# One layer norm's residual factor, made by GpSimd in a later step

## The chip, the cores and the metric

The kernel runs on one core of a Trainium2 chip. Its engines each have a queue of their own and meet only at semaphores: TensorE (PE; its weight loads are shown apart as PEld), VectorE (DVE), ScalarE (ACT), GpSimd (POOL) and SyncE (SP), which only issues DMAs. The metric is the device time of one execution in microseconds (us), as the median of several runs.

## The reference

The input is 32 sequences of 256 tokens with 128 values each. What is computed, cut to what matters:

```python
x = layernorm(x + attention(x))            # 16 heads of 64, causal softmax, output projection
mu, var = mean(x), var(x)                  # inside the second part, per token
xn = (x - mu) * rsqrt(var + 1e-5) * gamma + beta
probs = softmax(xn @ router_w.T / 1.5)     # 8 experts, the best two are kept
y = sum over the two experts: prob * (silu(xn @ W1[e]) @ W2[e])
out = layernorm(y + x)                     # x is the residual
```

The first layer norm and the one inside the second part are merged in the kernel: what goes to the experts is the doubly normed row z. The residual x is z times a factor for each token, which is worked out from the variance alone. This factor is what the change moves.

## The kernel before, in words

The kernel has three stretches: the attention, sequence by sequence (up to about 980 us), the experts on gathered blocks of 256 rows, and the last layer norm. Each engine's program is written out by hand, in order. In the attention every engine loops over n, the sequence (0 to 31), and q, the step (0 to 3), with d = 4n + q; a step treats two pairs of heads. There is no scheduler: what stands in `step(n, q, d)` of an engine is done in that order, and waits are semaphore counts.

The names that matter:

- PE, in a step: the scores of both pairs (L1292, L1295) into the PSUM banks ps_s, then projections for the next step (L1270), then the transposes of the step before's probabilities (L1313), again into ps_s. A pair's scores wait for two things: for ACT to have evacuated the pair's queries and keys (`qk_done`), and for the transposed probabilities that lie in the same bank to have been copied out (`pt_first_done`, `pt_second_done`).
- DVE: the masked maxima of the scores (L965, L969), the scaling of the probabilities by their reciprocal sums (L981 with 256 and L982 with 128 columns, both from SBUF to SBUF), and copies of transposed probabilities out of PSUM. In the last step of a sequence (q = 3) DVE copies the first pair's (L1149), in the other steps the second pair's (L1082).
- ACT: the exponentials (L691, L694), the evacuation of queries and keys (L680, L681), the copy of the attention outputs `ot` (L724), and in the last step the copy of the second pair's transposed probabilities (L773).
- POOL: in steps 0 and 2 it splits the outputs of two earlier steps into a rounded part (cast, L585, after ACT's copy L724) and a rest (L590). Between the first cast and the first L590 it waits for this step's scores. In step 0 it then works out the tokens' places among the experts (`slots`) and issues two indirect DMAs that send rows z to the experts' queues (L562). In step 1 it adds the bias to the input (L577) and sends the other two. In step 3 it waits for the statistics from DVE (L1049) and norms the rows (`norm`, L505 to L525).

`norm(n)` ends with two big instructions that write z (L517) and release `z_done`, and then four small ones that make the factor: a power (L520), two products (L521, L523) and the product that writes it into the KEEP column of z (L525), with `keep_done`. Each has 128 partitions by 2 elements. `send_tokens` waits for `keep_done`, one sequence behind.

Of the kernel before, what the change touches and what calls it, by code (L numbers as in the profile page):

```python
# [31 lines left out]
def postln_block(nc, x, wq, wk, wv, bq, bk, bv, wo, bo, gamma, beta, router_wt, w1, w2, out):  # L32
    SEQS, S, D = x.shape
# [26 lines left out]
    with ExitStack() as ctx:  # L60
# [6 lines left out]
        def sem(name):  # L67
            return ctx.enter_context(nc.semaphore(name))
# [213 lines left out]
        ln_link = sem("ln_link")  # L282
# [174 lines left out]
        def _(pool):  # L457
# [38 lines left out]

            LINKS = 8

            def norm(n):

                link = lambda k: (n - 1) * LINKS + k
                par = (n - 1) % 2
                mean, var = mv[:, :, 0], mv[:, :, 1]
                pool.wait_ge(mv_done, n)
                pool.tensor_scalar(ln_b[:], var, 1.0 + EPS, EPS * EPS, ALU.mult, ALU.add).then_inc(ln_link, 1)  # L505
                pool.tensor_tensor(ln_negmean[:], mean, neg_one[:, 0:TILES], ALU.mult).then_inc(ln_link, 1)
                pool.tensor_tensor(ln_a[:], var, eps_sb[:, 0:TILES], ALU.add).then_inc(ln_link, 1)
                pool.wait_ge(ln_link, link(3))
                pool.tensor_tensor(ln_r12[:], ln_b[:], neg_half[:, 0:TILES], ALU.pow).then_inc(ln_link, 1)
                if n >= 3:  # L510
                    pool.wait_ge(tokens_sent[par], (n - 1 - par) * (TILES * TOP * 8))
                pool.tensor_tensor(z[:, par, :, TOK], z[:, par, :, TOK], two_seqs[:], ALU.add)
                pool.wait_ge(ln_link, link(4))
                pool.tensor_tensor(ln_shift_z[:], ln_negmean[:], ln_r12[:], ALU.mult).then_inc(ln_link, 1)
                pool.wait_ge(ln_link, link(5))
                for i in range(TILES):
                    ins = pool.tensor_scalar(z[:, par, i, 0:D], res[:, i, :], ln_r12[:, i:i + 1],  # L517
                                             ln_shift_z[:, i:i + 1], ALU.mult, ALU.add)
                ins.then_inc(z_done, 1)
                pool.tensor_tensor(ln_r1[:], ln_a[:], neg_half[:, 0:TILES], ALU.pow).then_inc(ln_link, 1)  # L520
                pool.tensor_tensor(ln_br[:], ln_b[:], ln_r12[:], ALU.mult).then_inc(ln_link, 1)  # L521
                pool.wait_ge(ln_link, link(6))
                pool.tensor_tensor(ln_r1neg[:], ln_r1[:], neg_two[:], ALU.mult).then_inc(ln_link, 1)  # L523
                pool.wait_ge(ln_link, link(8))
                pool.tensor_tensor(z[:, par, :, KEEP], ln_br[:], ln_r1neg[:], ALU.mult).then_inc(keep_done, 1)  # L525

            def slots(n):
                pool.wait_ge(ranks_done, n - 1)
                for i in range(TILES):
                    ins = pool.tensor_tensor(slot_part[:, i], chosen[:, i],  # L530
                                             slot_if[:, i].unsqueeze(1).to_broadcast([P, TOP, E]), ALU.mult)
                ins.then_inc(slot_part_done, 1)
                pool.wait_ge(slot_part_done, n - 1)
                half = slot_part[:].rearrange("p i k (a e) -> p (i k) a e", a=2)
                pool.tensor_tensor(slot_four[:], half[:, :, 0], half[:, :, 1], ALU.add).then_inc(slot_link, 1)
                pool.wait_ge(slot_link, (n - 2) * 2 + 1)
                half = slot_four[:].rearrange("p k (a e) -> p k a e", a=2)
                pool.tensor_tensor(slot_two[:], half[:, :, 0], half[:, :, 1], ALU.add).then_inc(slot_link, 1)
                pool.wait_ge(slot_link, (n - 2) * 2 + 2)
                pool.tensor_tensor(slot_f[:].rearrange("p i k -> p (i k)"), slot_two[:, :, 0], slot_two[:, :, 1], ALU.add  # L540
                                   ).then_inc(slot_f_done, 1)
                pool.wait_ge(slot_f_done, n - 1)
                if n >= 4:
                    pool.wait_ge(tokens_sent[n % 2], (n - 2 - n % 2) * (TILES * TOP * 8))
                pool.tensor_copy(slot_now[:, n % 2, :], slot_f[:].rearrange("p i k -> p (i k)"))
                pool.wait_ge(z_done, n - 1)
                pool.tensor_copy(z[:, n % 2, :, SLOT], slot_f[:, :, 1])
                pool.wait_ge(gates_done, n - 1)
                pool.tensor_copy(z[:, n % 2, :, GATE], gates[:, :, 0])
                pool.tensor_tensor(z[:, n % 2, :, MORE], gates[:, :, 1], gates[:, :, 0], ALU.subtract  # L550
                                   ).then_inc(slots_done, 1)

            def send_tokens(n, i):
                par = n % 2
                if i == 0:
                    pool.wait_ge(slots_done, n - 1)
                    pool.wait_ge(keep_done, n - 1)
                    if n == SEQS - 1:
                        pool.wait_ge(tails_zeroed, 16 * E)
                for k in range(TOP):  # L560
                    col = i * TOP + k
                    pool.indirect_dma_start(  # L562
                        queue, bass.IndirectOffsetOnAxis(ap=slot_now[:, par, col:col + 1], axis=0),
                        z[:, par, i, :], None).then_inc(tokens_sent[par], 16)

            def rest_of_w1(e):
                pool.wait_ge(w1_hi_done, e + 1)
                pool.tensor_tensor(weights[:, W1_LO + e * HID:W1_LO + (e + 1) * HID], w1_raw[:, e], w1_part[:, e % 2],
                                   ALU.subtract).then_inc(w1_lo_done, 1)

            def residual_input(n):
                pool.wait_ge(bo_done, 1)
                if n >= 2:
                    pool.wait_ge(res_done, n - 1)
                pool.wait_ge(x_loaded[(n - 1) % 2], ((n - 1) // 2 + 1) * 16)
                for i in range(TILES):
                    ins = pool.tensor_tensor(xb[:, i, :], x_raw[:, (n - 1) % 2, i, :], bo_sb[:], ALU.add)  # L577
                ins.then_inc(xb_done, 1)

            def round_outputs(s):  # L580
                m, first = s // QUADS, s % QUADS * 2
                pool.wait_ge(ot_done, s + 1)
                if m >= 1:
                    pool.wait_ge(out_half_ready, 2 * m - (1 if first < 4 else 0))
                pool.tensor_copy(ot_hi[:, first:first + 2, :], ot[:, s % 2]).then_inc(ot_hi_done, 1)  # L585

            def rest_of_outputs(s):
                first = s % QUADS * 2
                pool.wait_ge(ot_hi_done, s + 1)
                pool.tensor_tensor(ot_lo[:, first:first + 2, :], ot[:, s % 2], ot_hi[:, first:first + 2, :].bitcast(F32),  # L590
                                   ALU.subtract).then_inc(ot_lo_done, 1)
# [7 lines left out]
            def step(n, q, d):  # L599
                if q in (0, 2) and n in MID:  # L600
                    round_outputs(d - 4)
                    pool.wait_ge(scores_ready, d * 2 + 1)
                    rest_of_outputs(d - 4)
                    round_outputs(d - 3)
                    rest_of_outputs(d - 3)
                if q == 0 and n - 1 in LATE:
                    slots(n - 1)
                    send_tokens(n - 1, 0)
                if q == 1 and n in MID:
                    pool.wait_ge(scores_ready, d * 2 + 1)  # L610
                    residual_input(n)
                if q == 1 and n - 1 in LATE:
                    send_tokens(n - 1, 1)
                if q == 3 and 2 <= n <= E + 1:
                    pool.wait_ge(scores_ready, d * 2 + 1)
                    rest_of_w1(n - 2)
                if q == 3 and n in MID:
                    norm(n)

            pool.wait_ge(small_loaded, 16 * 5)  # L620
            split_projection()
            sequences(step)
            for s in range(LAST - 4, LAST - 2):
                round_outputs(s)
# [5 lines left out]
                rest_of_outputs(s)  # L630
            residual_input(SEQS)
            send_tokens(SEQS - 1, 1)
            norm(SEQS)
            slots(SEQS)
            for i in range(TILES):
                send_tokens(SEQS, i)
# [24 lines left out]
            for f in range(FINS):  # L661
                par = f % 2
# [1009 lines left out]
```

## Time and profile before

| what | value |
|---|---|
| median of 3 runs | 1296.25 us (1296.0 to 1296.68) |
| the profiled execution's own time | 1294.77 us |
| its span in the profile | 1293.0 us |
| PE busy | 1268.1 us, 98% |
| ACT busy | 1136.9 us, 88% |
| DVE busy | 1038.6 us, 80% |
| POOL busy | 750.9 us, 58% |
| chain of work that ended last | PE 93%, ACT 2%, DVE 2%, DMA 2% |

How to read it: the span is what the profile covers, and the execution's own time holds a little around it. Busy shares are means over the three stretches. The chain follows the work back from the last instruction, at each step to what released it. In rows of a timeline the first number is the start in us from the span's beginning, the second the duration; several instructions of one line in a row are merged (x2). What is in brackets is the idle time of the engine before the row, and whose end released it. An instruction may start while the one before it on its engine is still finishing.

### The profile page before, as it was taken

What the parts mean: (1) busy time and instruction counts of PE and PEld (TensorE: products, weight loads), DVE (VectorE), ACT (ScalarE), POOL (GpSimd) and SP (SyncE); (2) the same over time, 40 slices, a digit from 0 to 9 for tenths busy, and PEclk for the clock granted to TensorE, in tenths of its full rate; (3) what the DMA queues carried; (4) which work ended last, traced back from release to release, by engine and by line L of the source; (5) the groups of instructions that cost most, each with busy time, mean ns of one, the idle gap of its engine ahead of it and who ended that gap; (6) DMA issues with size and microseconds to landing.
All of it is one profiled execution on the core that took longest, in us unless ns stands there. A gap on an engine that the chain in (4) does not pass through costs nothing.

```text
span 1293.0 us, 36146 instructions
## 1 busy us (share of the span) xinstructions
PE 1268.1 (98%) x11106; PEld 1125.8 (87%) x11106; DVE 1038.6 (80%) x5179; ACT 1136.9 (88%) x3514; POOL 750.9 (58%) x1333
## 2 busy tenths in 40 slices
PE   7999999999999999999999999999998999999997
PEld 6888888888888888888888888888886999999993
DVE  7888888888888888888888888888897765555537
ACT  7899999998998999889989999989887899999947
POOL 2246666666555565555665665555556676555545
PEclk9999999999999999999999999999999999999999
DMA  5000000000000000000000000000032233222228
GB/s 211 6 14 22 23 22 22 23 23 25 21 16 15 14 14 15 14 14 15 14 14 14 15 15 14 16 17 20 17 145 94 69 86 89 76 81 76 68 82 336
DMA packets 49213, 60.96 MB, mean 47 GB/s; under 512 B 8304, under 2 KB 35059, under 8 KB 48768
## 3 DMA queue, kind: packets, MB, share of 16 engines
q1 hardware_dynamic: 39376, 41.44, 9.9%
q0 software_dynamic: 8640, 17.13, 4.0%
q8 instruction: 93, 1.52, 0.5%
q14 instruction: 96, 0.79, 0.2%
q10 hardware_dynamic: 1008, 0.08, 0.1%
HBM read 30.72 MB, written 28.81 MB: 46 GB/s over the span
## 4 chain that ended last, share of the span: by engine, by line
PE 93%; ACT 2%; DVE 2%; DMA 2%; issue 1%; SPq 0%; POOL 0%; ACTq 0%; POOLq 0%; DVEq 0%
PE ps_a L1270 15%; PE ps_s L1313 13%; PE ps_s L1292 11%; PE ps_s L1270 8%; PE ps_f L1348 7%; PE ps_b L1305 7%; PE ps_f L1305 6%; PE ps_b L1564 5%; PE ps_a L1564 5%; PE ps_s L1295 4%; PE ps_b L1270 4%; PE ps_f L1270 3%; PE ps_s L1629 2%; PE ps_a L1369 1%; PE ps_s L1323 1%
## 5 line engine op out<-in xcount | busy, mean ns | idle before, releaser
L691 ACT ACTIVATE f_y<-f_y,neg_max 128x256 f32<-128x256 f32 x512 | 256.4, 501 | 46.8 <-DVE neg_max L965 46.7
L965 DVE CUSTOM_DVE_ANT_0 f_y<-ps_s,mask 128x256 f32<-128x256 f32 x512 | 214.6, 419 | 60.8 <-PE ps_s L1295 60.5
L1270 PE MATMUL ps_a<-xt_hi,weights 128*128 128x256 f32 x1024 | 240.2, 298 | 0.1
L590 POOL TENSOR_TENSOR ot_lo<-f_y,ot_hi 128x512 fp32r<-128x512 f32 x128 | 165.0, 1289 | 115.2 <-PE ps_s L1295 110.0
L981 DVE TENSOR_SCALAR f_y<-f_y,inv_sums 128x256 f32<-128x256 f32 x512 | 196.5, 384 | 7.0
L694 ACT ACTIVATE f_y<-f_y,neg_max 128x128 f32<-128x128 f32 x512 | 199.8, 390 | 0.0
L1313 PE MATMUL ps_s<-ident,f_y 128*128 128x128 f32 x1536 | 195.2, 273 | 0.0
L656 POOL DMA_INDIRECT y_tok<-f_y,m_dest x142 | 141.7, 998 | 84.8 <-DVE m_dest L1168 56.1
L1270 PEld LDWEIGHTS ps_a<-xt_hi,weights 128*128 128x128 f32 x1024 | 174.5, 188 | 16.0 <-issue 10.9
L1292 PE MATMUL ps_s<-qk 64*128 64x256 f32 x1024 | 176.4, 421 | 5.2 <-ACT qk L681 2.3
L1313 PEld LDWEIGHTS ps_s<-ident,f_y 128*128 128x128 f32 x1536 | 171.4, 141 | 4.9 <-issue 0.3
L982 DVE TENSOR_SCALAR f_y<-f_y,inv_sums 128x128 f32<-128x128 f32 x512 | 158.2, 309 | 0.0
L562 POOL DMA_INDIRECT queue<-z,slot_now x128 | 128.8, 1006 | 35.9 <-issue 26.1
L969 DVE CUSTOM_DVE_ANT_0 f_y<-ps_s,mask 128x128 f32<-128x128 f32 x512 | 146.5, 286 | 0.0
L1270 PE MATMUL ps_a<-xt_lo,weights 128*128 128x256 f32 x512 | 143.1, 279 | 0.0
L680 ACT ACTIVATE qk<-ps_a,bq_sb 128x256 f32<-128x256 f32 x256 | 119.3, 466 | 21.0 <-PE ps_a L1270 21.0
L1270 PE MATMUL ps_s<-m_xhi,weights 128*128 128x256 f32 x568 | 119.8, 293 | 3.1 <-DVE m_xlo L1193 1.8
L681 ACT ACTIVATE qk<-ps_a,bk_sb 128x256 f32<-128x256 f32 x256 | 119.3, 466 | 0.0
L585 POOL CAST ot_hi<-f_y 128x512 fp32r<-128x512 f32 x128 | 78.8, 616 | 62.9 <-ACT f_y L724 62.9
L1292 PEld LDWEIGHTS ps_s<-qk 64*128 64x128 f32 x1024 | 77.6, 185 | 37.9 <-issue 28.7
L1295 PEld LDWEIGHTS ps_s<-qk 64*128 64x128 f32 x1024 | 99.9, 187 | 10.9
L1295 PE MATMUL ps_s<-qk 64*128 64x128 f32 x1024 | 99.9, 271 | 0.0
(230 smaller groups left out, 3365.9 us busy)
## 6 DMA issues: line engine op xcount, KB each, us to landing
m_x<-queue SPq DMA_DIRECT2D x71, 133.0 KB
f_y<-y_tok SPq DMA_DIRECT2D x32, 256.0 KB, 6.8
queue<-empty SPq DMA_DIRECT2D x8, 532.0 KB, 3.8
x_raw<-in_x SPq DMA_DIRECT2D x32, 128.0 KB
out_x<-f_y SPq DMA_DIRECT2D x16, 256.0 KB, 6.3
y_tok<-f_y,m_dest POOLq DMA_INDIRECT x142
f_y<-in_w SPq DMA_DIRECT2D x1, 2048.0 KB, 11.7
m_w<-in_w SPq DMA_DIRECT2D x1, 2048.0 KB, 14.7
```

Source lines behind the costliest of these rows:

```text
L590: pool.tensor_tensor(ot_lo[:, first:first + 2, :], ot[:, s % 2], ot_hi[:, first:first + 2, :].bitcast(F32), ALU.subtract).then_inc(ot_lo_d ...
L691: act.activation(row[:, 0:2 * P], row[:, 0:2 * P], ACT.Exp, scale=-1.0, bias=neg_max[:, pair, h, 0:1], accum_out=sums[:, d % 2, pair, h, 0:1])
L694: act.activation(row[:, 2 * P:3 * P], row[:, 2 * P:3 * P], ACT.Exp, scale=-1.0, bias=neg_max[:, pair, h, 1:2], accum_out=sums[:, d % 2, pa ...
L965: dve.tensor_tensor_reduce(out=row[:, 0:2 * P], in0=ps_s[:, pair, h, 0:2 * P], in1=mask[:].rearrange("p a b -> p (a b)"), scale=-1.0, scal ...
L969: dve.tensor_tensor_reduce(out=row[:, 2 * P:3 * P], in0=ps_s[:, pair, h, 2 * P:3 * P], in1=mask[:, 1, :], scale=-1.0, scalar=-MASKED, op0= ...
L981: dve.tensor_scalar(row[:, 0:2 * P], row[:, 0:2 * P], inv_sums[:, d % 2, pair, h, 0:1], None, ALU.mult)
L982: ins = dve.tensor_scalar(row[:, 2 * P:3 * P], row[:, 2 * P:3 * P], inv_sums[:, d % 2, pair, h, 1:2], None, ALU.mult)
L1270: ins = pe.matmul(dst, lhs, rhs, start=(i == 0), stop=(i == len(terms) - 1))
L1292: pe.matmul(ps_s[:, pair, h, 0:2 * P], qk[r, pair, 0, P:2 * P], qk[r, pair, 1, :], start=True, stop=True)
L1295: ins = pe.matmul(ps_s[:, pair, h, 2 * P:3 * P], qk[r, pair, 0, 0:P], qk[r, pair, 1, 0:P], start=False, stop=True, skip_group_check=True)
L1305: ins = pe.matmul(dst_bank[r, cols], v[:, k, c * P + h * DH:c * P + (h + 1) * DH], pt[:, s % 2, pair, h, src], start=(k == 0), stop=(k == ...
L1313: ins = pe.transpose(ps_s[:, pair, h, dst:dst + P], probs[:, buf, pair, h, src:src + P], ident[:])
```

## The change

The four small instructions that make the factor leave `norm(n)` and become a function `keep_factor(n)`. In the loop POOL calls it for the sequence before in step 1, behind the second pair of DMA issues. After the loop it is called for norm 31 behind `send_tokens(SEQS - 1, 1)`, and for norm 32, the last, directly behind it, as before. The semaphore counts are the same. No other engine's program is changed.

```diff
             def norm(n):
-
-                link = lambda k: (n - 1) * LINKS + k
                 par = (n - 1) % 2
...
                 for i in range(TILES):
                     ins = pool.tensor_scalar(z[:, par, i, 0:D], res[:, i, :], ln_r12[:, i:i + 1],
                                              ln_shift_z[:, i:i + 1], ALU.mult, ALU.add)
                 ins.then_inc(z_done, 1)
+
+            def keep_factor(n):
+                par = (n - 1) % 2
+                pool.wait_ge(ln_link, link(n, 5))
                 pool.tensor_tensor(ln_r1[:], ln_a[:], neg_half[:, 0:TILES], ALU.pow).then_inc(ln_link, 1)
                 pool.tensor_tensor(ln_br[:], ln_b[:], ln_r12[:], ALU.mult).then_inc(ln_link, 1)
-                pool.wait_ge(ln_link, link(6))
+                pool.wait_ge(ln_link, link(n, 6))
                 pool.tensor_tensor(ln_r1neg[:], ln_r1[:], neg_two[:], ALU.mult).then_inc(ln_link, 1)
-                pool.wait_ge(ln_link, link(8))
+                pool.wait_ge(ln_link, link(n, 8))
                 pool.tensor_tensor(z[:, par, :, KEEP], ln_br[:], ln_r1neg[:], ALU.mult).then_inc(keep_done, 1)
...
                 if q == 1 and n - 1 in LATE:
                     send_tokens(n - 1, 1)
+                if q == 1 and n >= 2:
+                    keep_factor(n - 1)
...
             send_tokens(SEQS - 1, 1)
+            keep_factor(SEQS - 1)
             norm(SEQS)
+            keep_factor(SEQS)
             slots(SEQS)
```

The lines of POOL's program below the norm have numbers higher by 6 in the changed kernel up to the loop (the cast is L591 there, the rest L596, the sending DMA L568), and the factor's four are L526 to L531.

In POOL's program at the end of a sequence's last step and the start of the next sequence's first, before:

```order
L514 TENSOR_TENSOR ln_shift_z<-ln_negmean,ln_r12 128x2
L517 TENSOR_SCALAR z<-res,ln_r12,ln_shift_z 128x128 x2
L520 TENSOR_TENSOR ln_r1<-ln_a,neg_half 128x2
L521 TENSOR_TENSOR ln_br<-ln_b,ln_r12 128x2
L523 TENSOR_TENSOR ln_r1neg<-ln_r1,neg_two 128x2
L525 TENSOR_TENSOR z<-ln_br,ln_r1neg 128x2
L585 CAST ot_hi<-f_y 128x512
L590 TENSOR_TENSOR ot_lo<-f_y,ot_hi 128x512
L585 CAST ot_hi<-f_y 128x512
```

And the same place in the changed kernel:

```order
L516 TENSOR_TENSOR ln_shift_z<-ln_negmean,ln_r12 128x2
L519 TENSOR_SCALAR z<-res,ln_r12,ln_shift_z 128x128 x2
L591 CAST ot_hi<-f_y 128x512
L596 TENSOR_TENSOR ot_lo<-f_y,ot_hi 128x512
L591 CAST ot_hi<-f_y 128x512
```

The cast follows directly on the instructions that write z.

In POOL's program in the second step of a sequence, from the DMA issues that send rows to the cast of the third step, before:

```order
L562 DMA queue<-z,slot_now 67840x133 x2
L577 TENSOR_TENSOR xb<-x_raw,bo_sb 128x128 x2
L562 DMA queue<-z,slot_now 67840x133 x2
L585 CAST ot_hi<-f_y 128x512
L590 TENSOR_TENSOR ot_lo<-f_y,ot_hi 128x512
```

And the same place in the changed kernel:

```order
L568 DMA queue<-z,slot_now 67840x133 x2
L583 TENSOR_TENSOR xb<-x_raw,bo_sb 128x128 x2
L568 DMA queue<-z,slot_now 67840x133 x2
L526 TENSOR_TENSOR ln_r1<-ln_a,neg_half 128x2
L527 TENSOR_TENSOR ln_br<-ln_b,ln_r12 128x2
L529 TENSOR_TENSOR ln_r1neg<-ln_r1,neg_two 128x2
L531 TENSOR_TENSOR z<-ln_br,ln_r1neg 128x2
L591 CAST ot_hi<-f_y 128x512
L596 TENSOR_TENSOR ot_lo<-f_y,ot_hi 128x512
```

The four stand between the last DMA issue and the next cast.

## Rows read from the trace of the kernel before

**Rows 1.** Table of stretches: each engine's busy us and its instructions.

```profile
340.00:950.00 610.00, 610.00 (x5494) 532.81 (x5492) 533.94 (x2657) 548.61 (x1875) 354.54 (x697) 1.00 0.05 15
```

**Rows 2.** Waits, 340 to 980 us: us in total, times, longest.

```profile
POOL ot_lo L590 <- PE ps_s L1295: 74.1, 42, 2.2
```

**Rows 3.** Line 1149: duration ns min/median/max, and who waited for it.

```profile
L1149 DVE COPY pt<-ps_s x31: 945/950/954, 37.9 to 953.8; 128x768 f32<-128x768 f32 x31
...
  PE ps_s L1292: 0.8, 2
```

**Rows 4.** Timeline of POOL, 371 to 391 us.

```profile
371.86 0.69 POOL L520 TENSOR_TENSOR ln_r<-ln_a,neg_half 128x2 f32<-128x2 f32 x1
...
373.22 0.61 POOL L585 CAST ot_hi<-f_y 128x512 fp32r<-128x512 f32 x1
375.19 1.28 POOL L590 TENSOR_TENSOR ot_lo<-f_y,ot_hi 128x512 fp32r<-128x512 f32 x1 [1.36 <-PE ps_s L1295]
...
385.33 0.96 POOL L562 DMA_INDIRECT queue<-z,slot_now  x1 [0.30 <-issue]
387.55 0.61 POOL L585 CAST ot_hi<-f_y 128x512 fp32r<-128x512 f32 x1 [1.27 <-ACT f_y L724]
390.38 1.27 POOL L590 TENSOR_TENSOR ot_lo<-f_y,ot_hi 128x512 fp32r<-128x512 f32 x1 [2.22 <-PE ps_s L1295]
```

**Rows 5.** Timeline of ACT, 371 to 375 us.

```profile
371.60 0.57 ACT L724 ACTIVATE f_y<-ps_b 128x512 f32<-128x512 f32 x1
...
374.43 0.47 ACT L681 ACTIVATE qk<-ps_a,bk_sb 128x256 f32<-128x256 f32 x1
```

**Rows 6.** Timeline of DVE, 372 to 389 us.

```profile
372.21 0.28 DVE L982 TENSOR_SCALAR f_y<-f_y,inv_sums 128x128 f32<-128x128 f32 x1
372.41 0.35 DVE L981 TENSOR_SCALAR f_y<-f_y,inv_sums 128x256 f32<-128x256 f32 x1
...
372.87 0.95 DVE L1149 COPY pt<-ps_s 128x768 f32<-128x768 f32 x1
...
387.55 0.70 DVE L982 TENSOR_SCALAR f_y<-f_y,inv_sums 128x128 f32<-128x128 f32 x1
...
388.71 0.94 DVE L1082 COPY pt<-ps_s 128x768 f32<-128x768 f32 x1
```

**Rows 7.** Timeline of PE, 374 to 391 us.

```profile
374.17 0.70 PE L1292 MATMUL ps_s<-qk 64*128 64x256 f32 x4
...
374.95 0.70 PE L1292 MATMUL ps_s<-qk 64*128 64x256 f32 x4
...
375.81 0.73 PE L1270 MATMUL ps_b<-weights,xt_hi 128*128 128x512 f32 x2
...
390.14 0.70 PE L1292 MATMUL ps_s<-qk 64*128 64x256 f32 x4
```

**Rows 8.** Timeline of ACT at the end of sequence 0.

```profile
36.29 0.58 ACT L724 ACTIVATE f_y<-ps_b 128x512 f32<-128x512 f32 x1
```

**Rows 9.** Timeline of POOL, same place.

```profile
36.93 0.72 POOL L585 CAST ot_hi<-f_y 128x512 fp32r<-128x512 f32 x1 [20.89 <-ACT f_y L724]
```

**Rows 10.** Timeline of DVE, same place.

```profile
36.90 0.28 DVE L982 TENSOR_SCALAR f_y<-f_y,inv_sums 128x128 f32<-128x128 f32 x1
37.09 0.70 DVE L981 TENSOR_SCALAR f_y<-f_y,inv_sums 128x256 f32<-128x256 f32 x1
...
37.91 0.95 DVE L1149 COPY pt<-ps_s 128x768 f32<-128x768 f32 x1
```

**Rows 11.** Timeline of PE, same place.

```profile
39.00 0.70 PE L1292 MATMUL ps_s<-qk 64*128 64x256 f32 x4 [0.36 <-DVE pt L1149]
```

**Rows 12.** Timeline of PE at the start of sequence 31.

```profile
954.90 0.70 PE L1292 MATMUL ps_s<-qk 64*128 64x256 f32 x4 [0.42 <-DVE pt L1149]
...
956.41 0.73 PE L1270 MATMUL ps_b<-weights,xt_hi 128*128 128x512 f32 x2
```

**Rows 13.** Timeline of POOL, start of the last norm.

```profile
1006.65 0.19 POOL L505 TENSOR_SCALAR ln_b<-mv 128x2 f32<-128x2 f32 x1 [4.87 <-DVE mv L1049]
```

More of the change, by code:

```diff
@@ L497, in _, with link @@
             LINKS = 8
+            def link(n, k):
+                return (n - 1) * LINKS + k
             def norm(n):
-                link = lambda k: (n - 1) * LINKS + k
                 par = (n - 1) % 2
@@ L507, in norm @@
                 pool.tensor_tensor(ln_a[:], var, eps_sb[:, 0:TILES], ALU.add).then_inc(ln_link, 1)
-                pool.wait_ge(ln_link, link(3))
+                pool.wait_ge(ln_link, link(n, 3))
                 pool.tensor_tensor(ln_r12[:], ln_b[:], neg_half[:, 0:TILES], ALU.pow).then_inc(ln_link, 1)
@@ L512, in norm @@
                 pool.tensor_tensor(z[:, par, :, TOK], z[:, par, :, TOK], two_seqs[:], ALU.add)
-                pool.wait_ge(ln_link, link(4))
+                pool.wait_ge(ln_link, link(n, 4))
                 pool.tensor_tensor(ln_shift_z[:], ln_negmean[:], ln_r12[:], ALU.mult).then_inc(ln_link, 1)
-                pool.wait_ge(ln_link, link(5))
+                pool.wait_ge(ln_link, link(n, 5))
                 for i in range(TILES):
@@ L519, in norm @@
                 ins.then_inc(z_done, 1)
+            def keep_factor(n):
+                par = (n - 1) % 2
+                pool.wait_ge(ln_link, link(n, 5))
                 pool.tensor_tensor(ln_r1[:], ln_a[:], neg_half[:, 0:TILES], ALU.pow).then_inc(ln_link, 1)
                 pool.tensor_tensor(ln_br[:], ln_b[:], ln_r12[:], ALU.mult).then_inc(ln_link, 1)
-                pool.wait_ge(ln_link, link(6))
+                pool.wait_ge(ln_link, link(n, 6))
                 pool.tensor_tensor(ln_r1neg[:], ln_r1[:], neg_two[:], ALU.mult).then_inc(ln_link, 1)
-                pool.wait_ge(ln_link, link(8))
+                pool.wait_ge(ln_link, link(n, 8))
                 pool.tensor_tensor(z[:, par, :, KEEP], ln_br[:], ln_r1neg[:], ALU.mult).then_inc(keep_done, 1)
```

## The prediction

> **What bounds the kernel now.** I read the views from the coarse to the fine. The table of stretches comes first: from 340 to 950 us, twenty sequences of the attention, TensorE (PE) is busy all 610.00 us, GpSimd (POOL) only 354.54 [rows 1]. So time is won or lost there only where PE is made to wait. The list of waits is next: in the attention no row has PE, ScalarE (ACT) or VectorE (DVE) waiting for POOL. POOL waits for them, for one 74.1 us in front of L590 for PE's scores [rows 2]. A reader should conclude that moving four small POOL instructions cannot shorten PE's work directly, and then ask what else POOL's timing touches. For that one lays the timelines of POOL, ACT, DVE and PE beside each other at the two places of the change: from the last step of one sequence to the first of the next, and in the second step. I take the sequences that meet at 374 us; the pattern repeats every 30.5 us.
>
> **The place that is left.** Before, POOL makes the factor from 371.86 to the cast L585 at 373.22, so 1.36 us for four instructions [rows 4]. The cast has no use for being there: L590 behind it starts at 375.19, after 1.36 us of waiting for the scores. With the four gone POOL is free at 371.86, the cast then waits for ACT's copy of the outputs, L724, which ends at 371.60 + 0.57 = 372.17 [rows 5], and starts 0.05 to 0.06 us later, as it does behind the same copy elsewhere (36.29 + 0.58 = 36.87, cast at 36.93) [rows 8, 9]: at about 372.23, one microsecond earlier than before. L590 stays where the scores put it. By itself that is worth nothing.
>
> But at 372.23 DVE is scaling the probabilities (L982 at 372.21, L981 at 372.41, and on until 372.87), and at 373.22 it was not: it was copying from PSUM (L1149) [rows 6]. These scalings collide with casts. In the second step L982 starts at 387.55, in the same hundredth as a cast, and lasts 0.70 us instead of 0.28: 0.42 lost [rows 4, 6]. And the trace of before holds the coming situation once already: behind sequence 0 there is no norm, so its cast at 36.93 stands directly behind the copy. L982 started 0.03 earlier, at 36.90, and kept its time; the next L981 took 0.70 instead of 0.35, and from L982 to L1149 it is 37.91 - 36.90 = 1.01 us against 372.87 - 372.21 = 0.66: 0.35 lost [rows 6, 9, 10]. The small instructions that go away cost DVE nothing there: the scalings beside them have their short times.
>
> The Trainium skill, "SBUF — State Buffer", section "Who interferes with whom", says that DVE's tensor_scalar in a two-port mode and any GpSimd instruction take one port pair as a lock, that whoever starts first has it for the whole instruction, and that the other stands still. It speaks against this change, and the trace agrees on the collision and on who loses; on the size it does not: held for the cast's whole 0.61 us, L982 at 387.55 would have lasted 0.61 + 0.28 = 0.89 us, and it lasted 0.70.
>
> So L1149 ends 0.35 (DVE first, as behind sequence 0) to 0.42 us (cast first) later. The offset here, 0.01 to 0.02 us between L982 at 372.21 and the cast, lies between the 0.03 with which DVE won and the 0.00 with which the cast did; I take 0.35, because the same ACT and DVE instructions make the pattern at 36.9.
>
> **What that costs PE.** L1149 frees the PSUM bank for the next scores, and of 31 instances PE waited for 2 [rows 3]. When it does wait, the scores start 0.14 us behind its end (37.91 + 0.95 = 38.86, scores at 39.00) [rows 10, 11]. Normally they start at 374.17, 0.35 us behind its end at 373.82 [rows 6, 7]. The slack is 0.35 - 0.14 = 0.21 us. A delay of 0.35 makes the first pair's scores 0.14 late, one of 0.42 makes them 0.21 late.
>
> Most of that is given back at once. The second pair's scores at 374.95 start 0.05 us after ACT's L681 ends at 374.43 + 0.47 = 374.90, so they wait for ACT, not for the first pair; and from the first scores to the value projection behind them it is 375.81 - 374.17 = 1.64 us [rows 5, 7]. Where the scores did start late, it is 956.41 - 954.90 = 1.51 us [rows 12]. So 0.13 comes back: 0.14 - 0.13 = 0.01 us net for each sequence, or 0.21 - 0.13 = 0.08. With three readings rounded to 0.01 I take 0.03.
>
> **The second step.** There the four come behind the last DMA issue, which ends at 385.33 + 0.96 = 386.29. With their 1.36 us they end at 387.65; the cast starts at 387.55 now, after 1.27 us of idleness [rows 4]. It moves by 0 to 0.10 us. L590 behind it waits for scores until 390.38 anyway, so POOL's queue is not later at anything that others wait for. The cast's collision with DVE stays, at 0.35 to 0.45 us. Should it grow, L1082 ends at 388.71 + 0.94 = 389.65 and its bank is wanted at 390.14; with the 0.14 of above there are 0.35 us to spare [rows 6, 7]. If that cover were gone, each 0.1 us would cost 30 x 0.1 = 3 us. I count 0. The factor is read only by the DMA issues in the first step of the sequence after, and no DMA issue is moved.
>
> **The end of the attention.** The norm of the last sequence starts at 1006.65 after 4.87 us of waiting for the statistics [rows 13]. The factor of the one before, now in front of it, takes 1.36 of these: 0. Behind it nothing changes. What POOL does from 986 on starts up to 1.36 us earlier, and as PE waits for other things there, I count 0 with a bound of -1.4.
>
> **Sum.** The first steps of sequences 2 to 31 are touched, 30. For 29: 29 x 0.03 = 0.87. At the last of them PE already waits 0.42 us for L1149 [rows 12], so the whole 0.35 counts, and nothing comes back that was not back before. Together 1.2 us; with the cast first 29 x 0.08 + 0.42 = 2.7. The profiled execution took 1294.77 us (span 1293.0 and 1.77 around it) and would take 1296.0. The median of the runs is 1.48 above it, so 1296.25 + 1.2 = 1297.4.
>
> **The rivals.**
> - Nothing reaches DVE: the cast loses against the row of scalings and only POOL waits. For it: POOL has over a microsecond to lose. Against it: at 36.9 and 387.55 DVE paid both times. 1296.2.
> - Cast first, as at 387.55: 1296.25 + 2.7 = 1299.0, at the edge of what can be measured. The offset of 0.01 to 0.02 us decides.
> - Slower: the late scores are paid in full, because ACT's L681 shifts too or the second pair doesn't close up. Place: first scores of each sequence. It decides as soon as L1149 is over 0.21 us late. 29 x 0.14 + 0.35 = 4.4 to 29 x 0.21 + 0.42 = 6.5 us, 1300.7 to 1302.8. Against it stand rows 12, where they closed up.
> - The pair is held for the cast's whole length: 0.61 us late, 29 x (0.61 - 0.21 - 0.13) + 0.61 = 8.4 us, 1304.7. The 0.70 at 387.55 contradicts it. That is the rule of the skill's page named above.
> - Faster: POOL's earlier start from 986 on lets DVE and PE go earlier into the experts, up to -1.4 us, 1294.9; more would need a wait for POOL that the trace lacks.
>
> **How the numbers follow.** Forecast 0.50; nothing 0.20; cast first 0.13; paid in full 0.08; whole length 0.03; faster 0.06. A measurement of this kernel tells about 0.2%, 2.6 us, from no change. Forecast and nothing are within it, so is a part of cast first and most of faster: same 0.74, slower 0.21, faster 0.05. The range leaves out the ends, the 0.08 and 0.03 above and a part of faster below: 1295.3 to 1300.6; the forecast's own is 1296.4 to 1299.0.
>
> **What would show it.** Behind the norm of each sequence POOL's cast starts a microsecond earlier and one L981 or L982 of DVE lasts 0.70 us; L1149 starts 1.0 us behind the first L982; PE's waits name L1149 some 30 times at about 0.1 to 0.2 us each; from scores to value projection it is 1.51 us instead of 1.64, and a sequence takes 0.01 to 0.08 us more. I am wrong if the scalings keep 0.28 and 0.35, if ACT's L681 is late too, or if L1082 in the second step becomes what PE waits for.

## The result, and the profile after

| | median of 22 runs | lowest to highest |
|---|---|---|
| before | 1295.58 us | 1294.44 to 1298.76 |
| changed | 1297.8 us | 1294.38 to 1300.08 |

The ratio is 1.0014, with a 95% interval of 1.0008 to 1.0021: of 1295.6 us that is 1.8 us more, 1.0 to 2.7. (The two medians lie 2.2 us apart, inside that interval.) The prediction was 1.2 us more, which the interval holds too. The execution that was profiled took 1294.38 us, the lowest of the 22, so its span of 1292.6 us says nothing against that of before. What can be compared is how long the steps last.

The timeline of POOL of the changed kernel, at the same two places as [rows 4]; its cast is L591, the factor L526 to L531:

```profile
372.23 0.72 POOL L591 CAST ot_hi<-f_y 128x512 fp32r<-128x512 f32 x1 [0.36 <-ACT f_y L734]
375.31 1.29 POOL L596 TENSOR_TENSOR ot_lo<-f_y,ot_hi 128x512 fp32r<-128x512 f32 x1 [2.37 <-PE ps_s L1305]
...
385.51 0.96 POOL L568 DMA_INDIRECT queue<-z,slot_now  x1 [0.30 <-issue]
386.50 0.81 POOL L526 TENSOR_TENSOR ln_r<-ln_a,neg_half 128x2 f32<-128x2 f32 x1
...
387.92 0.72 POOL L591 CAST ot_hi<-f_y 128x512 fp32r<-128x512 f32 x1
390.38 1.29 POOL L596 TENSOR_TENSOR ot_lo<-f_y,ot_hi 128x512 fp32r<-128x512 f32 x1 [1.73 <-PE ps_s L1305]
```

The timeline of DVE, which answers to [rows 6]; the copies are L1159 and L1092 now, the scalings L991 and L992:

```profile
372.20 0.28 DVE L992 TENSOR_SCALAR f_y<-f_y,inv_sums 128x128 f32<-128x128 f32 x1
372.39 0.70 DVE L991 TENSOR_SCALAR f_y<-f_y,inv_sums 128x256 f32<-128x256 f32 x1
...
373.21 0.94 DVE L1159 COPY pt<-ps_s 128x768 f32<-128x768 f32 x1
...
388.10 0.63 DVE L992 TENSOR_SCALAR f_y<-f_y,inv_sums 128x128 f32<-128x128 f32 x1
388.65 0.95 DVE L1092 COPY pt<-ps_s 128x768 f32<-128x768 f32 x1
```

And that of PE, which answers to [rows 7]:

```profile
374.30 0.70 PE L1302 MATMUL ps_s<-qk 64*128 64x256 f32 x4
...
375.03 0.63 PE L1302 MATMUL ps_s<-qk 64*128 64x256 f32 x4
...
375.81 0.73 PE L1280 MATMUL ps_b<-weights,xt_hi 128*128 128x512 f32 x2
```

The cast stands at 372.23. L992 began 0.03 before it and kept its 0.28 us, L991 behind it took 0.70. From L992 to L1159 it is 373.21 - 372.20 = 1.01 us, where it was 0.66. L1159 ends at 374.15 and the scores start 0.15 behind it, not 0.35. And then the loss closes up: from the first scores to the value projection (L1280 into ps_b) it is 375.81 - 374.30 = 1.51 us, where it was 1.64.

The clearest reading is a table of steps. I took the start of the first scores (L1292, later L1302) of every step from PE's timeline, and the mean distance to those of the next step over sequences 3 to 28, in us; the runs below are in it too:

| kernel | step 0 | step 1 | step 2 | step 3 | sequence |
|---|---|---|---|---|---|
| before | 7.786 | 7.408 | 7.817 | 7.528 | 30.539 |
| before, second profile | 7.798 | 7.406 | 7.829 | 7.529 | 30.563 |
| changed | 7.656 | 7.406 | 7.831 | 7.674 | 30.567 |
| changed, second profile | 7.668 | 7.406 | 7.825 | 7.729 | 30.628 |
| factor at both places | 7.792 | 7.407 | 7.823 | 7.528 | 30.551 |
| factor in step 2 | 7.667 | 7.406 | 7.827 | 7.726 | 30.625 |
| cast after the copy | 7.787 | 7.407 | 7.818 | 7.530 | 30.542 |
| the same, second profile | 7.785 | 7.406 | 7.831 | 7.528 | 30.550 |
| the same with a small collision | 7.786 | 7.407 | 7.818 | 7.529 | 30.540 |
| changed, with a second cast | 7.659 | 7.407 | 7.821 | 7.966 | 30.853 |

Step 3 is 0.146 us longer, step 0 is 0.130 us shorter. Step 1, into which the factor went, is the same to 0.002 us. The last column wanders by 0.024 between two profiles of before, since steps 0 and 2 take one of two lengths 0.03 apart; the columns of steps 0 and 3 can be read without it.

### The profile page after: what moved, and what is told of

It is laid out like the page before. It is cut to its first block, busy times and chain, and to the rows that moved or that the text cites. A ratio compares the mean times of both kernels' runs of the same rounds, so it can differ in the third digit from the quotient of the medians.

```text
span 1292.6 us, 36146 instructions
## 1 busy us (share of the span) xinstructions
PE 1265.5 (98%) x11106; PEld 1126.0 (87%) x11106; DVE 1043.4 (81%) x5179; ACT 1137.1 (88%) x3514; POOL 759.0 (59%) x1333
## 4 chain that ended last, share of the span: by engine, by line
PE 92%; ACT 3%; DVE 2%; issue 1%; DMA 1%; POOL 1%; SPq 0%; ACTq 0%; POOLq 0%; DVEq 0%
PE ps_a L1280 15%; PE ps_s L1323 12%; PE ps_s L1302 11%; PE ps_s L1280 8%; PE ps_f L1358 7%; PE ps_b L1315 7%; PE ps_f L1315 6%; PE ps_b L1574 5%; PE ps_a L1574 5%; PE ps_s L1305 4%; PE ps_b L1280 4%; PE ps_f L1280 3%; PE ps_s L1639 2%; PE ps_a L1379 1%; ACT f_y L701 1%
## 5 line engine op out<-in xcount | busy, mean ns | idle before, releaser
L596 POOL TENSOR_TENSOR ot_lo<-f_y,ot_hi 128x512 fp32r<-128x512 f32 x128 | 165.3, 1291 | 131.5 <-PE ps_s L1305 126.2
L1280 PE MATMUL ps_a<-xt_hi,weights 128*128 128x256 f32 x1024 | 240.6, 298 | 0.0
L991 DVE TENSOR_SCALAR f_y<-f_y,inv_sums 128x256 f32<-128x256 f32 x512 | 205.7, 402 | 7.0
L1280 PEld LDWEIGHTS ps_a<-xt_hi,weights 128*128 128x128 f32 x1024 | 174.8, 188 | 16.0 <-issue 10.8
L1302 PE MATMUL ps_s<-qk 64*128 64x256 f32 x1024 | 174.3, 414 | 8.8 <-ACT pt L749 3.2
L992 DVE TENSOR_SCALAR f_y<-f_y,inv_sums 128x128 f32<-128x128 f32 x512 | 154.5, 302 | 0.0
L568 POOL DMA_INDIRECT queue<-z,slot_now x128 | 128.7, 1005 | 36.0 <-issue 26.2
L1280 PE MATMUL ps_a<-xt_lo,weights 128*128 128x256 f32 x512 | 143.1, 279 | 0.0
L1280 PE MATMUL ps_s<-m_xhi,weights 128*128 128x256 f32 x568 | 119.8, 293 | 2.9 <-DVE m_xlo L1203 1.7
L1302 PEld LDWEIGHTS ps_s<-qk 64*128 64x128 f32 x1024 | 79.0, 185 | 41.0 <-issue 31.9
L1305 PEld LDWEIGHTS ps_s<-qk 64*128 64x128 f32 x1024 | 102.4, 187 | 8.5
L591 POOL CAST ot_hi<-f_y 128x512 fp32r<-128x512 f32 x128 | 84.8, 663 | 39.0 <-ACT f_y L734 38.8
```

The costliest lines, as they stand in the source:

```text
L991: dve.tensor_scalar(row[:, 0:2 * P], row[:, 0:2 * P], inv_sums[:, d % 2, pair, h, 0:1], None, ALU.mult)
L992: ins = dve.tensor_scalar(row[:, 2 * P:3 * P], row[:, 2 * P:3 * P], inv_sums[:, d % 2, pair, h, 1:2], None, ALU.mult)
L1280: ins = pe.matmul(dst, lhs, rhs, start=(i == 0), stop=(i == len(terms) - 1))
L1302: pe.matmul(ps_s[:, pair, h, 0:2 * P], qk[r, pair, 0, P:2 * P], qk[r, pair, 1, :], start=True, stop=True)
L1305: ins = pe.matmul(ps_s[:, pair, h, 2 * P:3 * P], qk[r, pair, 0, 0:P], qk[r, pair, 1, 0:P], start=False, stop=True, skip_group_check=True)
```

## Experiments

Theory A: the early cast collides with DVE's scalings, which makes the copy in front of the next scores late. Rival B: the four instructions in step 1 cost the time, through the cast behind them. Rival C: the difference lies at the ends of the program. "Lateness" is how much later the copy starts behind the first 128-column scaling than the 0.66 us of before. "Attention" is the time from the first scores of sequence 1 to those of the last step: 979.62 - 39.00 = 940.62 us before, 980.49 - 38.71 = 941.78 in the changed kernel.

**The factor at both places.** Behind `z_done`, the four are done once more, into spare tiles (`dm_`):

```diff
                 ins.then_inc(z_done, 1)
+                if n < SEQS:
+                    pool.tensor_tensor(dm_r1[:], ln_a[:], neg_half[:, 0:TILES], ALU.pow).then_inc(dm_link, 1)
+                    pool.tensor_tensor(dm_br[:], ln_b[:], ln_r12[:], ALU.mult).then_inc(dm_link, 1)
+                    pool.wait_ge(dm_link, (n - 1) * 3 + 1)
+                    pool.tensor_tensor(dm_r1neg[:], dm_r1[:], neg_two[:], ALU.mult).then_inc(dm_link, 1)
+                    pool.wait_ge(dm_link, (n - 1) * 3 + 3)
+                    pool.tensor_tensor(dm_keep[:], dm_br[:], dm_r1neg[:], ALU.mult)
```

> The changed kernel, with the four small instructions done a second time directly behind the norm, into spare tiles that nobody reads, so that the cast of step 0 starts late again and the four in step 1 stay. Theory A (the early cast collides with VectorE's scalings and makes the copy in front of the scores late): the cast starts about 1.0 us behind the first 128-column scaling, no scaling in step 3 lasts 0.70 us, and from the first scores of sequence 1 to those of the last step it is 940.6 us as before (941.8 in the changed kernel); the time is that of before, 0 to 0.3 us more. Rival B (the four in step 1 cost the time, by pushing the cast of step 2): 941.8 us, 1.2 us or more above before. Rival C (the difference lies at the ends, not in the attention): the attention as in the changed kernel whatever is done.

Measured: ratio 0.9989 (0.9979 to 1.0), attention 940.91 us. Its POOL timeline has the spare four and then the cast, and its DVE timeline the short scalings:

```profile
371.71 0.68 POOL L528 TENSOR_TENSOR dm_r<-ln_a,neg_half 128x2 f32<-128x2 f32 x1
...
373.07 0.61 POOL L603 CAST ot_hi<-f_y 128x512 fp32r<-128x512 f32 x1
```

```profile
372.06 0.28 DVE L1004 TENSOR_SCALAR f_y<-f_y,inv_sums 128x128 f32<-128x128 f32 x1
372.26 0.35 DVE L1003 TENSOR_SCALAR f_y<-f_y,inv_sums 128x256 f32<-128x256 f32 x1
...
372.72 0.95 DVE L1171 COPY pt<-ps_s 128x768 f32<-128x768 f32 x1
```

The kernel does more work than the changed one, and the loss is gone: its interval and that of the changed kernel do not meet, and step 3 is back at 7.528. The work in step 1 is still there, so rival B falls. The four had served as a delay that kept the cast out of DVE's way.

**The factor in step 2.** The reverse: nothing is added in step 1.

```diff
-                if q == 1 and n >= 2:
+                if q == 2 and n >= 2:
                     keep_factor(n - 1)
```

> The changed kernel with the factor made in step 2, behind the roundings, where GpSimd then waits 6 us for the statistics, instead of step 1. Theory A: step 0 is as in the changed kernel, so 941.8 us from the first scores of sequence 1 to those of the last step, and the time is that of the changed kernel, 1 to 2 us above before. Rival B: the step-1 cost is gone, 940.6 us, the time of before.

Measured: ratio 1.0014 (1.0004 to 1.0023), attention 943.74 us. A's direction, B's is out again. But the attention is 2 us longer than expected: step 3 takes 7.726 us on average. The timelines of POOL and DVE show why:

```profile
373.21 0.61 POOL L591 CAST ot_hi<-f_y 128x512 fp32r<-128x512 f32 x1 [0.36 <-ACT f_y L734]
```

```profile
373.19 0.72 DVE L992 TENSOR_SCALAR f_y<-f_y,inv_sums 128x128 f32<-128x128 f32 x1
373.82 0.34 DVE L991 TENSOR_SCALAR f_y<-f_y,inv_sums 128x256 f32<-128x256 f32 x1
...
374.28 0.94 DVE L1159 COPY pt<-ps_s 128x768 f32<-128x768 f32 x1
```

Here the first L992 is the one that is blocked. The cast starts 0.02 us behind it, at 373.21, and wins. Then from L992 to L1159 it is 1.09 us instead of 1.01. By its timeline 17 of the 30 collisions go this way, which makes 17 x 0.08 = 1.4 of the 2 us.

**The cast after the copy.** It takes away the collision and leaves the factor in step 1. `pt_first_done` counts the copies of the first pair, `MID` are the sequences 1 to 31, and `round_outputs` begins with the cast:

```diff
                 if q in (0, 2) and n in MID:
+                    if q == 0:
+                        pool.wait_ge(pt_first_done, d - 1)
                     round_outputs(d - 4)
```

> The changed kernel, with the first cast of step 0 waiting until VectorE has copied the first pair's transposed probabilities; the factor stays in step 1. Theory A: the cast starts at about 1.6 us behind the first 128-column scaling and collides with none, the scores start 0.35 us behind the copy again, 940.6 us of attention, the time of before within 0.3 us (not below it by more than 0.4). Rival B: 941.8 us and 1.2 us above before.

Measured: ratio 0.9991 (0.9982 to 1.0), attention 940.95 us. The cast in POOL's timeline, and the scores in PE's:

```profile
373.64 0.61 POOL L591 CAST ot_hi<-f_y 128x512 fp32r<-128x512 f32 x1 [2.00 <-DVE pt L1161]
```

```profile
373.93 0.70 PE L1304 MATMUL ps_s<-qk 64*128 64x256 f32 x4
...
375.56 0.73 PE L1282 MATMUL ps_b<-weights,xt_hi 128*128 128x512 f32 x2
```

375.56 - 373.93 = 1.63 us, as before. The edit moves nothing but the cast, and step 3 is back at 7.530.

**A second cast.** It makes the suspected cost larger:

```diff
                 ins.then_inc(z_done, 1)
+                if n < SEQS:
+                    pool.tensor_copy(dm_copy[:], wo_sb[:, 0:4, :])
```

> The changed kernel with one more cast of 128x512 values, into a tile that nobody reads, directly behind each norm but the last: a second collision of the same size. Theory A with the slack of 0.21 us and 0.13 us given back: VectorE's copy is 0.70 to 0.84 us late instead of 0.36, the scores 0.49 to 0.63, net 0.36 to 0.50 for each of 29 sequences and 0.70 to 0.84 at the last: 11 to 15 us above before, 952 to 956 us of attention. If nothing is given back, 15 to 19 us. If the scalings are not blocked, or only GpSimd waits: as the changed kernel, 941.8 us. Rival B says the last as well.

Measured: ratio 1.0064 (1.005 to 1.0078), 8.3 us (6.5 to 10.1); attention 950.35 us, 9.7 above before. POOL's two casts, DVE's scalings and PE's scores:

```profile
374.15 0.60 POOL L524 CAST dm_copy<-wo_sb 128x512 fp32r<-128x512 f32 x1
374.71 0.67 POOL L594 CAST ot_hi<-f_y 128x512 fp32r<-128x512 f32 x1
```

```profile
374.26 0.65 DVE L994 TENSOR_SCALAR f_y<-f_y,inv_sums 128x256 f32<-128x256 f32 x1
374.83 0.63 DVE L995 TENSOR_SCALAR f_y<-f_y,inv_sums 128x128 f32<-128x128 f32 x1
375.38 0.34 DVE L994 TENSOR_SCALAR f_y<-f_y,inv_sums 128x256 f32<-128x256 f32 x1
...
375.84 0.94 DVE L1162 COPY pt<-ps_s 128x768 f32<-128x768 f32 x1
```

```profile
376.93 0.70 PE L1305 MATMUL ps_s<-qk 64*128 64x256 f32 x4 [0.37 <-DVE pt L1162]
```

Two collisions cost DVE (0.65 - 0.35) + (0.63 - 0.28) = 0.65 us, less than the 0.70 to 0.84 that I expected, so the time missed its range. The first loses only 0.30 us because its cast had begun 0.11 us before the scaling (374.15 and 374.26), so that less of it was left. With 0.65 the model holds: 0.65 - 0.21 - 0.13 = 0.31 net, 29 x 0.31 + 0.65 = 9.6 us, and the attention is 9.7 longer. Step 3 is 0.438 longer, which puts the slack at 0.65 - 0.438 = 0.21 us, and step 0 is again 0.127 shorter, so what comes back is a fixed amount and not a share.

**A small collision.** The kernel with the cast after the copy, and behind the norm:

```diff
                 ins.then_inc(z_done, 1)
+                if n < SEQS:
+                    pool.tensor_copy(dm_copy[:], wo_sb[:, 0:2, :])
```

> The kernel whose cast waits for VectorE's copy, with one cast of 128x256 values into a tile that nobody reads directly behind each norm but the last: a collision that should be smaller than the slack. Theory A: VectorE's copy is 0.10 to 0.20 us late, less than the slack of 0.21, so the scores start where they did, 940.6 to 941.0 us from the first scores of sequence 1 to those of the last step and the time of the kernel it is made from, within 0.4 us. A theory by which each lateness of the copy costs something: 29 x 0.10 to 0.20 = 3 to 6 us more.

Measured: ratio 0.9994 (0.9985 to 1.0003), attention 940.93 us. The added cast in POOL's timeline, DVE's scalings, then PE's scores:

```profile
371.18 0.39 POOL L524 CAST dm_copy<-wo_sb 128x256 fp32r<-128x256 f32 x1
```

```profile
371.28 0.43 DVE L996 TENSOR_SCALAR f_y<-f_y,inv_sums 128x256 f32<-128x256 f32 x1
371.64 0.28 DVE L997 TENSOR_SCALAR f_y<-f_y,inv_sums 128x128 f32<-128x128 f32 x1
...
372.29 0.95 DVE L1164 COPY pt<-ps_s 128x768 f32<-128x768 f32 x1
```

```profile
373.51 0.70 PE L1307 MATMUL ps_s<-qk 64*128 64x256 f32 x4
```

The collision costs DVE 0.43 - 0.35 = 0.08 us, a little less than expected. The scores stand 0.27 us behind the copy's end at 373.24, and PE loses nothing: step 3 is 7.529. So this lateness of 0.08 us, inside the slack, is free.

**The changed kernel again.**

> The changed kernel once more, to see whether the toss between cast and scaling falls another way in another execution. If always VectorE first: 941.8 us of attention again. If some fall to the cast, as in the kernel with the factor in step 2: each such sequence 0.08 us more, so 941.8 to 944.2 us, and the time 1.2 to 3.4 us above before.

Measured: ratio 1.0015 (1.0006 to 1.0024), attention 943.57 us. The same program now shows both outcomes. One that went to the cast, in the timelines of POOL, DVE and PE:

```profile
403.73 0.61 POOL L591 CAST ot_hi<-f_y 128x512 fp32r<-128x512 f32 x1 [0.36 <-ACT f_y L734]
```

```profile
403.70 0.72 DVE L992 TENSOR_SCALAR f_y<-f_y,inv_sums 128x128 f32<-128x128 f32 x1
404.35 0.34 DVE L991 TENSOR_SCALAR f_y<-f_y,inv_sums 128x256 f32<-128x256 f32 x1
...
404.80 0.94 DVE L1159 COPY pt<-ps_s 128x768 f32<-128x768 f32 x1
```

```profile
405.89 0.70 PE L1302 MATMUL ps_s<-qk 64*128 64x256 f32 x4 [0.16 <-DVE pt L1159]
...
407.40 0.74 PE L1280 MATMUL ps_b<-weights,xt_hi 128*128 128x512 f32 x2
```

By the timeline 19 of 30 have the longer lateness here, and none in the first profile. (One more in each profile, at the end of sequence 29, went to the cast with a smaller loss.) Each costs 0.08 us more than the other outcome. The cast itself tells who came first: it lasts 0.71 or 0.72 us where the 128-column scaling in front of it kept its time (372.23 in the first profile), and 0.61 where it held that scaling up (403.73 here). In all 30 places of both profiles the two signs agree. The view of line 1159 says it too, in its row on who waited for the copy (us, times), first of the changed kernel's first profile:

```profile
  PE ps_s L1302: 0.5, 2
```

And of this one:

```profile
  PE ps_s L1302: 3.5, 20
```

**Two controls.** The kernel before against itself, and the cast after the copy a second time.

> The kernel before against itself: the ratio shows how far two programs that are the same measure apart. Expected 1.000, and no more than 0.0010 off; 940.6 us of attention.

> The kernel whose cast waits for VectorE's copy, once more, beside the kernel before measured against itself. If it is really faster than before, the ratio is 0.999 again and the kernel before's own is not; if not, both are the same distance from 1. Attention 940.6 to 941.0 us in either case.

Measured: 0.9997 (0.9985 to 1.0009) and 1.0002 (0.9993 to 1.0011); attention 941.39 and 941.13 us. Both attentions are a little longer than expected. The 0.999 of two kernels above, 1.4 and 1.2 us less than before and below what was expected of them, is not shown to be a gain: the one of them that was repeated gave 1.0002. No kernel here is shown to beat the one before. The control also shows that the attention of before itself differs by 0.77 us between two profiles, so a difference of attentions below about 1 us proves nothing by itself, and the steps have to be read.

PE's clock is not the cause of the changed kernel's loss either: the mean granted clock over the executions of its second series was 0.9975, as over those of before in the same series.

Rival C is not needed: step 3 is longer wherever the early cast meets the scalings, and nowhere else. What the attention of the changed kernel takes more than the first profile of before is 1.2 us in one profile and 3.0 in the other (0.4 and 2.2 against the second), on either side of the 1.8 us measured. The stretches behind it, from the last step's scores to the end, took 313.36 and 313.59 us in the profiles of before and 312.10 and 312.83 in those of the changed kernel. That they are shorter by up to 1.5 us is left open; such ends vary between 311.97 and 314.93 over all the kernels here, and the two kernels with the cast after the copy, the same program, have 314.29 and 311.97.

## Why the prediction was right

- **The place.** Right. The cast at 372.23 was predicted to the hundredth, and the loss is DVE's, as predicted, and not POOL's. The experiment that moves only the cast removes it.
- **The collision.** Right in size for DVE first, 0.35 us of lateness, and for the other outcome, 0.42 predicted and 1.09 - 0.66 = 0.43 measured. The choice between them was half right: the profile of the changed kernel took the first, a second one the other in 19 of 30. I chose by an offset of hundredths, and the same 0.03 us stands with either outcome (372.20 and 372.23; 403.70 and 403.73). "Cast first" was set aside as a rival with 0.13, and it is part of the normal behaviour. By the table of steps the first profile's mix comes to 29 x (0.146 - 0.130) + 0.36 = 0.8 us and the second's to 29 x (0.201 - 0.118) + 0.44 = 2.8. The 1.8 us measured lies between, so this mix can be why it is above 1.2; that it is, is not shown, since nothing tells the mix of the other executions. That the forecast came out inside the interval is in that much luck.
- **Slack and what comes back.** Right in size: 0.21 us of slack, 0.13 given back. The second cast measured both by itself; the small collision shows only that 0.08 us lies within the slack. The reason given for the 0.13 covers a part of it. The second pair starts 375.03 - 374.30 = 0.73 us behind the first and no longer 374.95 - 374.17 = 0.78, so 0.05 comes from the wait for ACT that is gone. The other 0.08 lies behind the second pair's start (375.81 - 375.03 = 0.78 against 375.81 - 374.95 = 0.86), and why is not shown.
- **The rule on the lock.** The Trainium skill's "SBUF — State Buffer", section "Who interferes with whom", says that a DVE instruction in a two-port mode and a GpSimd instruction contend for a shared pair of ports, that whoever issues first has it for the whole instruction, and that the other stands still. The traces agree on the collision, and that either engine can be the one that is held: the scalings, or the cast by 0.72 - 0.61 = 0.11 us. On the size they do not, by recorded durations: a cast's whole 0.61 us would be lost, and the scalings held by such casts lost 0.30 to 0.44. No run here shows in which mode the scalings run.
- **The second step.** The cost was right, nothing; the way there was not. I said the cast moves by 0 to 0.10 us, and it moved by 387.92 - 387.55 = 0.37. Of the 0.27 beyond, 0.18 is that the DMA issues before it are later themselves (385.51 against 385.33), and the rest comes with the power, which took 0.81 us there and not 0.69. L1092 still started at 388.65, earlier than the 388.71 of before: the cast met a later scaling, which lost 0.63 - 0.28 = 0.35 us and not 0.42.
- **The last sequence.** Right. PE already waited for the copy there [rows 12], and I counted the whole 0.35 us. The rows are the first scores of the last step of sequence 30, first in the kernel before, then in the changed kernel, and there also those of sequence 31:

```profile
946.88 0.70 PE L1292 MATMUL ps_s<-qk 64*128 64x256 f32 x4
```

```profile
947.50 0.70 PE L1302 MATMUL ps_s<-qk 64*128 64x256 f32 x4
...
955.88 0.70 PE L1302 MATMUL ps_s<-qk 64*128 64x256 f32 x4 [0.78 <-ACT qk L691]
```

That step lasts 954.90 - 946.88 = 8.02 us before and 955.88 - 947.50 = 8.38 in the changed kernel: 0.36 more. (The bracket names ACT, but 955.88 is also 0.15 behind the copy's end, as elsewhere.) It is 8.46 in the changed kernel's second profile, where this collision went to the cast, 8.67 with the second cast, and 8.10 with the small collision. Without slack the copy's lateness is paid in full, even the 0.08.

- **What would be seen.** Wrong in one point: I expected some 30 waits that name the copy. The view counts 2 in one profile and 20 in the other; scores at 374.30 that stand 0.15 us behind the copy's end have no wait in their row. Counting named waits would have missed most of the first profile's collisions.

## What to carry to other kernels

The engines' programs meet only at semaphores, but their instructions can also meet without one. An engine that nobody waits for can still hold up another by when it starts: before work is moved off an engine, look at what then moves forward behind it and which instructions of the neighbour that falls on. Small instructions that stand in front of a big GpSimd instruction for other reasons can be the delay that keeps it off VectorE's scalings; if the order changes, a wait in front of it can give the same protection, as the cast after the copy did. And where one early instance in the old trace already has the new order, as sequence 0 had here, it gives the size of the effect: 0.35 us here, though one instance did not show that the other outcome, 0.43, would occur as well.

## What the runs showed of the hardware that was not expected

- Recorded starts this close do not tell who wins a collision: casts that started 0.02 to 0.03 us behind a 128-column scaling sometimes blocked that scaling (lateness 0.43 us) and sometimes only the next one (0.35 us), in one and the same program.
- One sum fits the size of every collision shown here: the scaling that is held ends as if it had begun 0.19 to 0.21 us before the recorded end of the cast. Behind sequence 0 [rows 9, 10] the cast ends at 36.93 + 0.72 = 37.65, and the scaling as if begun at 37.09 + 0.70 - 0.35 = 37.44. In the same way it is 372.95 and 372.74 in the changed kernel, 404.34 and 404.14 with the cast first, 374.75 and 374.56 with the second cast, 371.57 and 371.36 with the small one. Over the ten profiles 410 of 421 lengthened scalings that overlap a cast lie between 0.18 and 0.22; the other 11 are at the end of the attention, from 968 us on. So a cast has no fixed price: what counts is how much of it is left when the scaling comes, without its last 0.2 us. Why those do not count is not shown.
- Not every GpSimd instruction costs VectorE something: the four with 2 elements for each partition stood beside the scalings in the kernel with the factor at both places, and these kept 0.28 and 0.35 us. A cast of 256 columns, begun 0.10 us before the scaling, cost 0.08 us; casts of 512 columns cost 0.30 to 0.44.
- Scores that start late take 1.51 us with their second pair instead of 1.64, whether 0.15 us late (changed kernel) or 0.44 (with a second cast: 376.93 to 378.44).
